# A Mamba block beside a sparse expert layer on one core: rows added to a DRAM accumulator by transfers, experts over 13 chunks

## The reference

```python
rn = xn * rsqrt(mean(xn * xn, -1) + EPS) * norm_w
skip, x_in = rn @ skip_w.T, rn @ in_w.T              # 256 -> 512
x1 = silu(conv_b + causal 4-tap convolution of x_in)
delta = softplus(x1 @ wd1.T @ wd2.T + wd2_b)
h_l = exp(delta_l * A) * h_(l-1) + (delta_l * x1_l) * B_l   # 512 channels x 16 states, over 1024 steps
y = (sum over states of h * C + x1 * W_D) * silu(skip)
mamba = xn + y @ out_w.T                             # its own residual

gates = softmax(xn @ Wr)                             # 8 experts
inds = the 2 experts with the SMALLEST gates; scores = their gates / their sum
moe = sum over the 2 of score * (silu(xn @ W1[e]) * (xn @ V1[e])) @ W2[e]
```

## Time and profile before

| | |
|---|---|
| median of three runs | 1481.36 us |
| span of the profiled execution | 1480.3 us |
| PE busy | 1279.1 us, 86% |
| DVE busy | 1243.6 us, 84% |
| ACT busy | 915.7 us, 62% |
| POOL busy | 868.9 us, 59% |
| DRAM read, written | 49.46 MB, 35.39 MB |

### The profile page before, as it was taken

The page is one execution under the profiler, slowest core; times in us unless marked ns, Lnnn a source line. Parts: engine busy times, 40 slices in busy tenths (PEclk is TensorE's granted clock), DMA queues, the critical chain, the costliest instruction groups (busy, mean ns, idle before and its releaser), DMA issues.

```text
span 1480.3 us, 24598 instructions
## 1 busy us (share of the span) xinstructions
PE 1279.1 (86%) x7476; PEld 1028.4 (69%) x7476; DVE 1243.6 (84%) x2066; ACT 915.7 (62%) x2017; POOL 868.9 (59%) x1284
## 2 busy tenths in 40 slices
PE   4686674999999999999999999999999999865765
PEld 3575553777778777777778777777878777754654
DVE  6787876889797888889797888889797898999996
ACT  3776676576675757566675757566575756755330
POOL 0332477766668585766758585666758545335563
PEclk8797877999999999999999999999999999976876
DMA  9400826000000000001000000001000100144232
GB/s 316 144 2 0 291 97 211 17 25 24 29 23 30 29 23 22 29 23 30 26 26 30 30 22 23 26 26 30 23 29 30 30 23 15 49 133 133 74 112 84
DMA packets 76093, 86.43 MB, mean 58 GB/s; under 512 B 9920, under 2 KB 67136, under 8 KB 75968
## 3 DMA queue, kind: packets, MB, share of 16 engines
q1 hardware_dynamic: 69536, 68.02, 14.4%
q0 software_dynamic: 6144, 16.79, 3.8%
...
HBM read 49.46 MB, written 35.39 MB: 57 GB/s over the span
## 4 chain that ended last, share of the span: by engine, by line
PE 65%; DVE 21%; issue 6%; ACT 3%; POOL 2%; DMA 1%; DVEq 0%; POOLq 0%; SPq 0%; ACTq 0%
PE bps L818 12%; PE hps L827 11%; DVE hb L1058 9%; PE bankH L941 8%; PE bankX L971 8%; PE bankV L963 8%; PE bankG L850 3%; DVE yac L1072 3%; PE bankG L948 2%; PE bankG L860 2%; PE bankV L903 2%; PE bankG L863 2%; PE bankH L903 2%; PE bankV L850 1%; DVE tok L1255 1%
## 5 line engine op out<-in xcount | busy, mean ns | idle before, releaser
L1058 DVE TENSOR_TENSOR_SCAN hb<-aexp,carry,bps 128x256 f32<-128x256 f32 x768 | 509.8, 726 | 89.8 <-PE bps L818 71.5
L515 ACT ACTIVATE aexp<-delta,Am 128x256 f32<-128x256 f32 x1024 | 440.0, 503 | 60.9 <-DVE hb L1058 54.9
L1072 DVE SCALAR_TENSOR_TENSOR yac<-hps,BC,yac 128x512 f32<-128x512 f32 x480 | 334.7, 738 | 27.6 <-PE hps L827 27.4
L818 PE MATMUL bps<-idn,ub 128*128 128x128 f32 x2048 | 298.4, 290 | 62.7 <-DVE hb L1058 44.7
L827 PE MATMUL hps<-idn,hb 128*128 128x128 f32 x2048 | 292.1, 288 | 49.2 <-DVE yac L1072 44.7
L827 PEld LDWEIGHTS hps<-idn,hb 128*128 128x128 f32 x2048 | 250.6, 149 | 101.1 <-issue 79.0
L713 POOL TENSOR_SCALAR ub<-uT,BC 128x512 f32<-128x512 f32 x448 | 312.6, 710 | 11.8 <-ACT uT L602 10.5
L818 PEld LDWEIGHTS bps<-idn,ub 128*128 128x128 f32 x2048 | 250.3, 149 | 99.4 <-issue 59.5
L799 POOL COPY carry<-hb 128x4 f32<-128x4 f32 x256 | 55.7, 218 | 232.8 <-DVE hb L1058 231.2
L1058 DVE TENSOR_TENSOR_SCAN hb<-aexp,bps 128x256 f32<-128x256 f32 x256 | 154.6, 666 | 41.6 <-PE bps L818 37.9
L775 POOL TENSOR_TENSOR vs<-g,vs 128x512 f32<-128x512 f32 x72 | 91.9, 1276 | 166.2 <-ACT vs L665 165.3
...
## 6 DMA issues: line engine op xcount, KB each, us to landing
...
tok<-xbuf SPq DMA_DIRECT2D x72, 128.0 KB, 2.2
ybuf<-tok SPq DMA_DIRECT2D x72, 128.0 KB, 1.7
w<-in_W SPq DMA_DIRECT2D x2, 4096.0 KB, 24.0
...
tok<-in_x SPq DMA_DIRECT2D x32, 128.0 KB, 2.2
```

The lines of the kernel that those rows point to most:

```text
L515: nc.scalar.activation(aexp[:, u % 2, e, :], delta[:, c % 2, e, :], ACT.Exp, scale=Am[:, e, n:n + 1]).then_inc(s_a, 1)
L818: mm = pe.transpose(bps[q][:, i * CH + s * P:i * CH + (s + 1) * P], ub[:, u % 2, s, e * P:(e + 1) * P], idn[:, :])
L1058: v.tensor_tensor_scan(hb[:, u % 2, e, :], aexp[:, u % 2, e, :], bps[e // 2][:, (e % 2) * CH:(e % 2 + 1) * CH], first, ALU.mult, ALU.add). ...
L1072: ins = v.scalar_tensor_tensor(out=yac[:, c % 2, s, :], in0=hps[s][:, :], scalar=scale, in1=yac[:, c % 2, s, :], op0=ALU.mult, op1=ALU.add)
```

## The change

**Where rows are summed.** `mbuf` and `ybuf` are replaced by one DRAM array `acc` of 4096 + 128 rows. In chunk 0 POOL computes `x + xn` for each token tile (`resid`, one multiply-add of 128x256 each) and SP stores it to `acc`, two tiles a transfer. Each Mamba sub-block is added to its rows by a direct transfer with addition, issued by POOL (O3); each expert tile by an indirect transfer with addition, to the rows of its tokens (FC). The token's row number and its weight travel with the dispatched row: rows of `xbuf` have 258 elements, `wid` holds the pairs, and ACT writes two copies into the ring by a broadcast, with a second small copy for the pair. An empty slot has the weight zero and a row number in the last 128 rows. ACT weights the rows when it copies them out. Each transfer with addition waits on POOL until the one before it has landed (`wait_added`). POOL also turns the row numbers of a tile to integers (`idx`).

**The end.** There are no S pieces. In chunk 15 SP copies the finished rows of `acc` to the output, DRAM to DRAM (CP, two transfers); the last two sub-blocks are added on DVE to rows read from `acc` (LL, O3) and stored.

**The order.** Experts go over chunks 2 to 14, six tiles in chunks 2 to 8 and five in 9 to 14 (`FFN_TILES`). The last tile's third product is in chunk 15. All place tables are new. A table `LATER` sets some pieces some places later on one engine: on POOL FC by 2, O3 by 2, FB by 1, O1 by 4, O2 by 1. The convolutions of chunks 1, 14 and 15 go from DVE to POOL; ACT makes one product of two in chunk 1 and none in chunk 14. The ring has 6 double slots where it had 8 single ones; input tiles have four slots where they had two. The zero fill of `xbuf` and the stores to `acc` alternate on SP in chunk 0.

```diff
+FFN_TILES = {c: 6 if c < 9 else 5 for c in range(2, 15)}
-DVE_CONV = (0, 1, 2, 14, 15)
-ACT_PRODUCTS = {1: 2, 14: 2}
+DVE_CONV = (0, 2)
+ACT_PRODUCTS = {1: 1}
...
+LATER = {
+    "PE": {"B5": 1},
+    "ACT": {"B3": 1},
+    "DVE": {},
+    "POOL": {"O2": 1, "O1": 4, "FC": 2, "O3": 2, "RES": 3, "FB": 1},
+    "SP": {"FA": 2, "FC": 1},
+}
...
+        def wait_added(eng, piece):
+
+            at_least(eng, added, 16 * ADDS[piece])
+
+        def wait_landed(eng, piece):
+
+            at_least(eng, added, 16 * (ADDS[piece] + 1))
...
+                elif kind == "R" and piece[1] < TT // 2:
+                    i = piece[1]
+                    if i < 8:
+                        sp.wait_ge(id_set, 4)
+                        a0, a1 = i * JT // 8, (i + 1) * JT // 8
+                        sp.dma_start(xbuf.rearrange("(a p) d -> p a d", p=P)[:, a0:a1, :],
+                                     empty.unsqueeze(1).to_broadcast([P, a1 - a0, ROW])).then_inc(zeroed, 16)
+                    sp.wait_ge(res_set, 2 * (i + 1))
+                    sp.dma_start(acc[2 * i * P:2 * (i + 1) * P, :].rearrange("(s p) d -> p s d", p=P),
+                                 resid[i % 2]).then_inc(res_out[i % 2], 16)
...
+                elif kind == "CP":
+                    t0, t1 = ((0, TT - 2 * SUB), (TT - 2 * SUB, TT - SUB))[piece[1]]
+                    wait_landed(sp, ("FC", JT))
+                    wait_landed(sp, ("O3", 1, CHUNKS - 3 + piece[1]))
+                    sp.dma_start(out_rows[t0 * P:t1 * P, :], acc[t0 * P:t1 * P, :]).then_inc(o_out, 16)
...
-                        nc.scalar.activation(ring[t % RING], xall[:, t, :], ACT.Identity, bias=nmr[:, t:t + 1],
-                                             scale=rstd[:, t:t + 1]).then_inc(xn_r, 1)
+                        nc.scalar.activation(ring[t % RING][:, :, 0:D], xall[:, t, :].unsqueeze(1).to_broadcast([P, TOPK, D]),
+                                             ACT.Identity, bias=nmr[:, t:t + 1], scale=rstd[:, t:t + 1])
+                        nc.scalar.activation(ring[t % RING][:, :, D:ROW], wid[:, t, :, :], ACT.Copy).then_inc(xn_r, 1)
...
+                elif kind == "FC" and piece[1] > 0:
+                    j = piece[1] - 1
+                    pool.wait_ge(ld_xs[j % SLOTS_IN], 16 * (j // SLOTS_IN + 1))
+                    if j >= 2:
+                        wait_landed(pool, ("FC", j - 1))
+                    nc.gpsimd.tensor_copy(idx[:, j % 2:j % 2 + 1], tin[:, j % SLOTS_IN, D + 1:D + 2]).then_inc(idx_set, 1)
+                    pool.wait_ge(idx_set, j + 1)
+                    wait_taken(pool, "X", piece)
...
+                    wait_added(pool, piece)
+                    nc.gpsimd.indirect_dma_start(
+                        out=acc, out_offset=bass.IndirectOffsetOnAxis(ap=idx[:, j % 2:j % 2 + 1], axis=0),
+                        in_=tout[:, j % 2, :], in_offset=None, compute_op=ALU.add).then_inc(added, 16)
...
+                    wait_added(pool, piece)
+                    nc.gpsimd.dma_start(acc[t * P:(t + 1) * P, :], mst[:, s, :], accum_op=ALU.add).then_inc(added, 16)
...
-                elif kind == "S":
-                    t = piece[1]
-                    i = t % 2
-                    mamba = sbuf_m[i]
...
-                        v.scalar_tensor_tensor(out=sbuf_m[i], in0=gbuf[i][:, k * D:(k + 1) * D], scalar=wt[:, t:t + 1],
-                                               in1=sbuf_m[i], op0=ALU.mult, op1=ALU.add).then_inc(sums, 1)
```

319 lines of the change are left out of this document (160 added, 159 removed), and 15 rows, old and new, of tables (B_PLACES, F_PLACES).

## The result

The changed kernel takes **1543.2 us** (median of four runs, 1541.21 to 1546.86). The kernel before took 1482.11 in the runs beside it. The ratio is 1.0417, with a 95% interval of 1.04 to 1.0433. The change makes the kernel 4% slower, where 5% faster was forecast; the time is far outside the range given.

A forecast was written before the change was run, and what follows sets the result against it. PE was taken to bound chunks 2 to 13 and DVE chunks 14 and 15. The terms 52.7 + 95.4 + 107.5 + 7 x 84.7 + 6 x 79.3 + 83.0 gave a span of 1407.3, so 1408 us; range 1374 to 1450.

The forecast's parts named there:

- the stall of PE in a six-tile chunk: Chunks 2 to 8: PE stands 0.8 us waiting for POOL's products, making a six-tile chunk 84.7 us (bounds 82.5 and 89).
- The dense point: POOL's order in a six-tile chunk, from the third convolution to the products of unit 11: 24.0 us of operations, adds included.
- The stretch is 24.0 + 2(L - 1.3): POOL's time at the crowded place of a six-tile chunk, two adds waiting for landings: 29.0 us; PE stands for the excess.
- L: Time from the issue of an add to its landing: 3.8 us taken, between 3.0 and 5.2.
- PE's 28.2: Six-tile chunk: 28.2 us of PE's own work, two tiles included, before it needs POOL's products of unit 11.
- moderate queue: Rival: POOL's queue of adds, landing in 5.2 us, stalls PE 4.8 us in a six-tile chunk; whole 1442; chance 0.18.
- scattered waits: Five-tile chunks: direct adds stand apart from expert adds, so 1.2 us is given for waits, making 79.3 us a chunk.
- 83.9 - 5.8 = 78.1 us, if PE stays the limit.: Five-tile chunks, 9 to 14: one expert tile fewer takes its 5.8 us of PE time off the chunk.
- I take 5.0 of the 8.9 us: Chunk 0: moving chunk 1's convolution from DVE to POOL saves 5.0 us, giving 95.4 (bounds 91.5 and 103).
- 13 units x 0.71 = 9.2 us: Chunk 1: ACT products moved to POOL before its last dispatch; +3.0 us taken in all, giving 107.5 (bounds 101.5 and 116).
- Chunk 14: Counted as one of six five-tile chunks at 79.3 us; it also loses its sums.
- 80.7 + 2.3 = 83.0: Chunk 15: 80.7 us without the sums, plus 2.3 for a late instruction fetch during the DRAM-to-DRAM copy (bounds 79 and 91).

## Why the prediction was wrong, step by step

Three steps failed as mechanisms: the stall of PE in a six-tile chunk (0.8 us put, 4.9 measured on average, and a cost of the clock behind it that the sum didn't have), the start (priced by sums of work, lost by order), and the saving of a left-out tile (5.8 us put, 2.0 measured without adds).

**The dense point: right in its form, 3.3 us short, and without its consequence.** "The stretch is 24.0 + 2(L - 1.3)" gave 29.0 us on POOL. In chunk 3 it runs from 419.87 to 452.21, 32.3 us. L itself was right: 3.9 us for an expert add and 3.2 for a direct one, where 3.8 was taken. So was the chain: from the first direct add to the products (441.07 to 450.28) 9.2 us, forecast 2 x 1.3 + 1.3 + 0.2 + 2 x 2.5 = 9.1. What was short are the ordinary operations between: from start to next start the two convolutions take 5.5 and 4.9 us where the earlier trace rows price 4.15 each (+ 2.1), and the four product pairs 6.7 where 5.5 was put (+ 1.2). 0.5 of the 2.1 isn't new: an undisturbed convolution takes 4.4 us by its starts before the change as well, because the earlier trace rows give durations without the gaps between them. With plain writes in place of the adds the same two take 5.0 and 4.4, so 1.0 goes with the addition; the last 0.5 falls on the first of the two, which stands beside DVE's stretched X2 in both kernels (see the end). The slow operations stand behind an indirect add. Its record (1.63 us) laps over the next operation by 0.56 us, though that one starts 1.07 us behind it with the addition or without; the lost time shows at an operation further on. An expert add with its cast takes 1.5 us of the queue, as was put. With PE's 28.2 the stall becomes 4.1 when the measured stretch is put in, and is 4.7. That is the rival "moderate queue" in size, but by another term than L.

**The step that was missing is PE's clock.** In the sum for a six-tile chunk a stall costs only itself. In chunk 3, 4.7 us of idling are followed by 2.9 us lost at the lower clock: 3.9 + 2.9 = 6.8 us of the 10.0 by which it is over its forecast. Over the seven chunks the stall is 4.9 us on average, and from the end of each of these stops on the granted clock is at its lower level for 3.4 or 6.8 us; half of PE's busy time in these stretches, 2.1 us on average, is what that costs (an estimate from the traced clock). Together 4.1 + 2.1 = 6.2 us of the 8.6 by which a six-tile chunk is over its forecast. Moving the two adds apart gives back 43 of the 60.4 us of the seven chunks, and no lower clock stands in chunks 3 to 8 of that kernel.

**The adds cost something beside the stall.** With them apart a six-tile chunk takes 87.1 us, with none on POOL 84.3. Part of it is seen as waits: in chunk 3 the wait of PE behind POOL's `xc` (1.0 us) and the one behind DVE's X2 (0.6) stay with the adds apart, and neither stands in the list of the chunk of 84.7 us. PE's busy time is 0.9 us longer as well (83.2 for 82.3). The prediction had "scattered waits" only for five tiles; these 2.8 us are most of the rest of the item. The time that the adds take on POOL was forecast well (11.6 us; 68.6 against 56.4 busy without them, 12.2).

**"83.9 - 5.8 = 78.1 us, if PE stays the limit."** It doesn't. Without any add on POOL the five-tile chunk takes 82.3 us on average of chunks 9 to 13. The busy time of PE falls by 4.8 us for a tile, where 5.8 was put, and PE's waits grow from 2.2 us in the six-tile chunk to 4.8 in the five-tile one; why the busy time falls by less stays open. The price of a tile was read where PE runs without a gap. The likely reason for the waits is that some units are left with less PE work than the 3.9 to 4.2 us of DVE, or the 6.0 of POOL in a unit with a convolution, need; no run shows this alone. The comparison of sums (DVE 71 of 84) can't show it; a table of the 16 units could. The 1.2 us for the adds in this chunk was right: 83.6 against 82.3.

**Chunk 0, "I take 5.0 of the 8.9 us".** The sum of work was right and beside the point. DVE's busy time fell from 84.5 to 76.5 and the chunk grew by 14 us. What was moved besides work was order: three router pieces at the first place. The prediction priced what each engine does in the chunk, and not what stands ahead of the first units. With the old places, the convolution on DVE and the rest of the new work the chunk takes 97.5 to 102.5 us, about the 100.4 of before; so the 5.0 us did not come off.

**Chunk 1, "13 units x 0.71 = 9.2 us".** POOL's part was priced as a length of its queue. What counts is what a product waits for in it: one product behind a clump of dispatches let PE stand 14.8 us. With both products on ACT the chunk takes 111.7 us, with the old places too 107.2. That this is close to the 107.5 forecast is luck: the forecast was for another division of the products.

**Chunk 14** was put with the other five-tile chunks, without a look at its own tables: + 15.9 us. 11 of them went: 2.5 with the adds apart and 8.5 with its own tables and the start.

**Chunk 15, right.** 80.7 + 2.3 = 83.0 forecast, 82.0 measured, DVE busy 70.3 (68 said). The copy from DRAM to DRAM hides. The 2.3 us for a late fetch didn't come as such: no stop of DVE by "issue" stands in the list of this chunk, and no run shows that such a stop is a fetch. DVE had 2 us more to do instead, so this part of the agreement is luck.

Of the 134 us the two adds in a row are 43 in the six-tile chunks, the start 35, chunk 14 11; the remaining 45 are the five-tile step (21), the rest of the six-tile chunks (17) and smaller parts. A gain is there, but a small one. With the orders repaired it is 1.4 to 1.7%; with the adds left out altogether, and so without their result, 3.4%.
